# First edges of a GNN's nodes: 64 fixed rows of sorted destinations per window, marked and summed on TensorE, in place of a histogram and one row gather per window; edge gathers two for each finished one-hot

## The reference

```python
edge_index = jnp.stack([src, dst])              # 206250 edges, sorted by dst, 6250 nodes, 64 features
h = jnp.maximum(_layernorm(x), 0.0)
x = x + _L0_gnn_ref(h, edge_index, ...)         # two GIN convolutions
h = jnp.maximum(_layernorm(x), 0.0)
x = x + _L1_gnn_ref(h, edge_index, ...)         # message MLP, segment sum, update MLP

def _gin_conv(x, src, dst, Wa, ba, Wb, bb):
    agg = jax.ops.segment_sum(x[src], dst, num_segments=N)
    return jax.nn.relu((x + agg) @ Wa + ba) @ Wb + bb
```

## Time and profile before

| | |
|---|---|
| median of 3 runs | 957.7 us |
| profiled execution (its span) | 940.74 us (938.9 us) |
| PE busy | 873.5 us, 93% of the span |
| DVE busy | 699.8 us, 75% |
| ACT busy, POOL busy | 480.2 us, 401.3 us |
| `build` ends at | 386 us |
| indirect DMAs | 98, of which 49 are row gathers |

### The profile page before, as it was taken

The page is one execution under the profiler, slowest core; times in us unless marked ns, Lnnn a source line. Parts: engine busy times, 40 slices in busy tenths (PEclk is TensorE's granted clock), DMA queues, the critical chain, the costliest instruction groups (busy, mean ns, idle before and its releaser), DMA issues.

```text
span 938.9 us, 25210 instructions
## 1 busy us (share of the span) xinstructions
PE 873.5 (93%) x11282; PEld 709.5 (76%) x11282; DVE 699.8 (75%) x656; ACT 480.2 (51%) x573; POOL 401.3 (43%) x281
## 2 busy tenths in 40 slices
PE   0589999999999999899999999999999989999996
PEld 0258888988999999778777677777777867777774
DVE  7789999999999999384555555665545676778773
ACT  2655646554545554364545455445454455554551
POOL 5878888887000000304536656540010144454450
PEclk9969999999999999999999999999999999999998
DMA  3024344344333444315434334443442466788871
GB/s 111 18 87 132 106 154 152 106 135 152 109 123 123 140 140 140 134 34 163 121 114 130 110 116 121 134 125 105 124 119 63 138 200 204 238 233 242 244 215 48
DMA packets 81857, 126.86 MB, mean 135 GB/s; under 512 B 10288, under 2 KB 58544, under 8 KB 81616
## 3 DMA queue, kind: packets, MB, share of 16 engines
q1 hardware_dynamic: 78608, 121.98, 43.1%
q0 software_dynamic: 3136, 3.22, 1.5%
HBM read 84.22 MB, written 40.94 MB: 133 GB/s over the span
## 4 chain that ended last, share of the span: by engine, by line
PE 52%; DVE 4%; ACT 1%; issue 1%; POOL 0%; DVEq 0%; POOLq 0%; ACTq 0%
PE net_ps_hi L1271 15%; PE net_ps_lo L1271 14%; PE net_ps_lo L1288 7%; PE net_ps_hi L1288 7%; PE net_ps_mt L1214 5%; PE net_ps_ft L1214 2%; DVE net_wide L833 1%; PE net_ps_check L1306 1%; DVE hT L926 1%; DVE hT L921 1%; ACT net_wide L1110 1%; DVE net_first L933 1%; PE net_ps_mt L1318 0%; POOL net_wide L879 0%; PE net_ps_mt L1358 0%
## 5 line engine op out<-in xcount | busy, mean ns | idle before, releaser
L1271 PE MATMUL net_ps_hi<-net_wide,net_first 128*128 128x512 f32 (+1 forms) x637 | 248.4, 394 | 1.3 <-POOL net_wide L879 1.3
L1271 PE MATMUL net_ps_lo<-net_wide,net_first 128*128 128x512 f32 (+1 forms) x637 | 240.8, 382 | 0.0
L833 DVE CAST net_wide<-net_raw 128x3584 fp32r<-128x3584 uint8 (+1 forms) x90 | 202.4, 2257 | 42.1 <-PE net_ps_lo L1288 16.3
L1110 ACT ACTIVATE net_wide<-net_raw 128x3584 fp32r<-128x3584 uint8 (+1 forms) x64 | 193.6, 3025 | 78.1 <-PE net_ps_lo L1271 44.9
L338 DVE TENSOR_TENSOR build_hot_lo<-build_grid_lo,build_keys_t 128x4096 bf16<-128x4096 bf16 x100 | 225.1, 2283 | 2.9 <-PE build_ps_cnt L569 2.9
L589 PE MATMUL build_ps_out<-build_parts_pad,build_cnts 128*128 128x195 bf16 x2401 | 223.3, 250 | 2.8 <-ACT build_cnts L456 1.2
L456 ACT ACTIVATE build_cnts<-build_ps_cnt 128x980 uint16<-128x980 f32 (+3 forms) x176 | 151.3, 900 | 128.1 <-PE build_ps_cnt L569 125.6
L589 PEld LDWEIGHTS build_ps_out<-build_parts_pad,build_cnts 128*128 128x128 fp8e4 x2401 | 202.5, 98 | 8.5 <-issue 4.0
L1271 PEld LDWEIGHTS net_ps_hi<-net_wide,net_first 128*128 128x128 f32 x637 | 119.8, 188 | 31.8 <-issue 7.0
L1271 PEld LDWEIGHTS net_ps_lo<-net_wide,net_first 128*128 128x128 f32 x637 | 119.9, 188 | 24.7 <-issue 2.6
L833 POOL CAST net_wide<-net_raw 128x3584 fp32r<-128x3584 uint8 (+1 forms) x28 | 84.8, 3028 | 106.2 <-PE net_ps_hi L1288 52.5
(11 more groups left out here) (171 smaller groups left out, 709.2 us busy)
## 6 DMA issues: line engine op xcount, KB each, us to landing
net_raw<-edge_counts SPq DMA_DIRECT2D x168, 448.0 KB, 3.8
edge_counts<-build_cnts SPq DMA_DIRECT2D x168, 224.0 KB
xres<-in_x SPq DMA_DIRECT2D x1, 1568.0 KB, 7.1
net_raw<-edge_counts SPq DMA_DIRECT2D x14, 112.0 KB, 2.0
out<-xres SPq DMA_DIRECT2D x12, 128.0 KB, 4.2
build_rows<-in_dst_rows,build_row_i POOLq DMA_INDIRECT x49
build_edges<-in_edges,build_start_i POOLq DMA_INDIRECT x49
edge_counts<-build_cnts SPq DMA_DIRECT2D x7, 112.0 KB
```

Of the source, the lines that this page charges most:

```text
L833: return issue(expanded[e % WIDE_RING][:, 0:n, :, :].rearrange("p w a d -> p (w a d)"), raw[e % RAW_RING][:, 0:n, :, :].rearrange("p w a d ...
L1110: expand(act, lambda to, x: nc.scalar.activation(to, x, ACT.Identity), e).then_inc(grown["act"], 1)
L1271: last = nc.tensor.matmul(ps[(b + 1) % 2][:, 0:n * P], first[:, c, lo:lo + H], expanded[e % WIDE_RING][:, 0:n, k, :], start=(c == 0), stop ...
```

## The change

The host now also passes, for each window w, 64 rows of sorted destinations around row 33 w - 15 (`rows`), and the row ahead of each of them (`rows_before`). They are loaded by plain DMAs from SP, two of 32 KB for pair 0 and two of 768 KB for the other pairs; two windows lie on the two halves of the partitions. x is loaded by ACT's queue in four pieces. DVE marks which pivots a node has passed (`past`, bf16) and subtracts each row from the next (`jump`). PE multiplies the jumps by the marks, which adds up to the row in which the node's first edge lies less the node's own number (`select_rows`, L614 and L620), ACT takes the sign (`sign_rows`, L475), two matmuls of one column per window count (`rank_rows`, L631 and L632), and DVE adds the span's base (`find_starts`, L319). This goes in ten looks: one pair, two pairs, then three pairs each. All ten stand ahead of the first `count`.

All row gathers, the compares and the histogram are gone. The edge gather of window w waits, from w = 4 on, until (w - 3) / 2 one-hots, rounded up, are finished.

```diff
+def look(k):
+    if k < 2:
+        return (slice(0, 1), slice(1, LOOK))[k]
+    return slice(LOOK * (k - 1), min(LOOK * k, NU))
+def found_with(w):
+    return w // 2 // LOOK + 1 if w > 1 else 0
+def asked_behind(w):
+    return -(-(w - AT_ONCE + 1) // 2)
...
-                sp.dma_start(xin, a["x"].rearrange("p (w f) -> p w f", f=F)).then_inc(x_in, 16)
+                for i, u in enumerate((look(0), slice(1, NU))):
+                    sp.dma_start(span_rows[:, u, :], a["rows"].rearrange("p (u e) -> p u e", e=P)[:, u, :]).then_inc(span_in[i], 16)
+                    sp.dma_start(span_before[:, u, :], a["rows_before"].rearrange("p (u e) -> p u e", e=P)[:, u, :]).then_inc(span_in[i], 16)
...
+                def gather_edges(g, lo, hi):
                     for w in range(lo, hi):
-                        nc.gpsimd.indirect_dma_start(rows[:, w, :], None, a["dst_rows"],
-                                                     bass.IndirectOffsetOnAxis(ap=row_i[:, w:w + 1], axis=0)
-                                                     ).then_inc(rows_in[g], 16)
+                        if w == lo or found_with(w) != found_with(w - 1):
+                            pool.wait_ge(starts_known, found_with(w) + 1)
+                        if w >= AT_ONCE:
+                            pool.wait_ge(hot_ready, asked_behind(w))
...
+                def pass_pivots(u):
+                    shape = [P, u.stop - u.start, P // 2, 2]
+                    v.tensor_tensor(past[:, u, :].rearrange("p u (k t) -> p u k t", t=2),
+                                    grid_lo[:, :].rearrange("p (k t) -> p k t", t=2)[:, None, :, :].broadcast_to(shape),
+                                    piv_off[:, u, None, :].broadcast_to(shape), ALU.is_gt).then_inc(passed, 1)
+                def row_jumps(i, u):
+                    dve.wait_ge(span_in[i], 32)
+                    v.tensor_tensor(jump[:, u, :], span_rows[:, u, :], span_before[:, u, :], ALU.subtract).then_inc(jumps, 1)
+                def find_starts(k):
+                    u, turns = look(k), min(2, NW - 2 * look(k).start)
+                    by_pair = [t[:, :].rearrange("p (u t) -> p t u", t=2)[:, 0:turns, u] for t in (start_i, span_base)]
+                    dve.wait_ge(ranked, k + 1)
+                    v.tensor_tensor(by_pair[0], ps_start[k % CNT_RING][:, 0:turns, 0:u.stop - u.start], by_pair[1], ALU.add
+                                    ).then_inc(starts_known, 1)
...
+                def sign_rows(k):
+                    u = look(k)
+                    n, turns = u.stop - u.start, min(2, NW - 2 * u.start)
+                    act.wait_ge(selected, k + 1)
+                    nc.scalar.activation(sign[:, 0:turns, u, :], ps_cnt[k % CNT_RING][:, 0:turns, 0:n * P].rearrange("p t (u e) -> p t u e", e=P),
+                                         ACT.Sign, bias=half[:, 0:1]).then_inc(signed, 1)
...
+                for i, w in enumerate(shares):
+                    act.dma_start(xin[:, w, :], a["x"].rearrange("p (w f) -> p w f", f=F)[:, w, :]).then_inc(x_in[i], 16)
+                act.wait_ge(consts, 7)
+                nc.scalar.activation(warm[:, :], half[:, :], ACT.Sign)
+                for k in range(0, 3):
+                    sign_rows(k)
+                copy_first_keys(0)
+                for k in range(3, LOOKS):
+                    sign_rows(k)
                 for q, w in enumerate(shares):
                     act.wait_ge(centred, q + 1)
                     nc.scalar.activation(tmp[:, w, :], h64[:, w, :], ACT.Square).then_inc(squared, 1)
-                copy_first_keys(0)
-                compare_rows(1)
...
+                def select_rows(k):
+                    u = look(k)
+                    n = u.stop - u.start
+                    if k >= CNT_RING:
+                        pe.wait_ge(starts_known, k - CNT_RING + 1)
+                    if k == 5:
+                        pe.wait_ge(keys_copied, 1)
+                    pe.wait_ge(passed, 1 + (k > 0))
+                    turns = min(2, NW - 2 * u.start)
+                    for t in range(turns):
+                        nc.tensor.matmul(ps_cnt[k % CNT_RING][:, t, 0:n * P].rearrange("p (u e) -> p u e", e=P), lane_share[:, :],
+                                         grid_lo[:, None, :].broadcast_to([P, n, P]), start=True, stop=False)
+                    pe.wait_ge(jumps, 1 + (k > 0))
+                    for j in range(n):
+                        for t in range(turns):
+                            e = slice(t * ROWS, (t + 1) * ROWS)
+                            last = nc.tensor.matmul(ps_cnt[k % CNT_RING][:, t, j * P:(j + 1) * P], jump[e, u.start + j, :],
+                                                    past[e, u.start + j, :], start=False, stop=(j == n - 1))
+                    last.then_inc(selected, 1)
+                def rank_rows(k):
+                    pe.wait_ge(signed, k + 1)
+                    for w in range(2 * look(k).start, min(2 * look(k).stop, NW)):
+                        u, t = divmod(w, 2)
+                        e = slice(t * ROWS, (t + 1) * ROWS)
+                        to = ps_start[k % CNT_RING][:, t, u - look(k).start:u - look(k).start + 1]
+                        nc.tensor.matmul(to, sign[:, t, u, :], minus_half[:, :], start=True, stop=False)
+                        last = nc.tensor.matmul(to, past[e, u, :], row_step[e, :], start=False, stop=True)
+                    last.then_inc(ranked, 1)
...
+                for k in range(0, 3):
+                    select_rows(k)
+                    rank_rows(k)
+                pe.wait_ge(consts, 15)
                 turn_keys(0, first_keys[0]).then_inc(first_turned, 1)
+                for first in range(3, LOOKS, 3):
+                    for k in range(first, min(first + 3, LOOKS)):
+                        select_rows(k)
+                    for k in range(first, min(first + 3, LOOKS)):
+                        rank_rows(k)
...
+                pe.wait_ge(starts_known, LOOKS)
                 count_first(0, 2)
```

213 lines of the change are left out of this document (85 added, 128 removed).

## The result

The changed kernel has a median of 957.5 us over 20 runs (949.1 to 967.9), the kernel before one of 949.2 us over 20 (939.3 to 970.0). The ratio is 1.0108, 95% interval 1.0074 to 1.0142: slower, by about 10 us. That is clear of the noise, though under the 2% that the prediction took for the least that can be told. The ratio compares the undisturbed executions alone, so it is not quite that of the two medians. The forecast was no change. Its number, 957.5, is the measured median to 0.1 us, but by luck: it was the old median of 957.7 over three runs with nothing added, and over twenty runs that median is 949.2. As differences, the range of 8 in 10 was -9.5 to +9.5 us, and the measurement lies just outside. The profiled execution took 951.66 us, with a span of 949.3 us, against 940.74 and 938.9.

What follows compares the result with a forecast made beforehand. DVE's chain was taken to set the end of `build`: start 69.3 + steady part 291.2 + tail 24.6 = 385.1 us against 385.15, `net` unchanged. So the median was forecast at 957.5 us, with 8 in 10 from 948 to 967.

Steps and rivals of the forecast that it cites:

- What bounds the kernel: `build`: DVE's chain sets the end, 385.15 us before the change; PE is faster after the gathers and waits.
- rival B: Late parts of x: first `use` at 71.7, PE's chain ends at 389.2, 4 us slower, up to 10; chance 0.20.
- Steps 1 to 4: Start, first look to span 0's keys: first starts 8.3, second rows 13.5, `row_jumps` 1.7, keys done at 22.1 us.
- Steps 5 and 6: Start: means and centring, three looks' starts at 28.0, a one-hot quarter, looks 6 to 9 done at 34.0 us.
- T2: Start of pair 2's `hot_a` on DVE: forecast 69.3 us, 4.1 later than before (65.24).
- Steps 7 and 8: Start, from 34.0 to 69.3 us: squares, scaling, keys and one-hot quarters, with 2.0 of waiting for the keys' copy.
- The clock: PE in the start: 1.2 GHz granted from 54.8 to 65 us; no higher clock counted on from the added matmuls.
- The steady part's gain: DVE, pair 2 to 24: 295.27 less 2.9 of waits for PE and 1.2 of `find_starts` gives 291.2 us.
- Pacing at 0: Edge gathers' wait for one-hots: four gathers at 3.1 us at most, 12.4 us, costed at 0 on DVE.
- Rival D: Edge gathers' wait for one-hots starves DVE of edges: some 3 us, 5 spans, +10 to +15 us; chance 0.03.
- Rival A: Start: earlier rows, no wait for keys' copy, full clock; T2 at 64.1, 5.2 us faster, up to 9; chance 0.22.
- C: PE's loss is not the gathers': its chain keeps 324.1 us and ends at 389.1, 4 slower; chance 0.10.

Runs made afterwards that it cites:

- `ranks_grouped`: Changed kernel with each look's `sign` matmuls (128 rows of weights) first, then all `past` ones (64 rows): `build` ends at 382.1 us, ratio 1.0043.
- `ranks_tall`: Changed kernel with the second rank matmul also given 128 rows of weights, step 0 on the other window's rows: `build` ends at 384.1 us, ratio 1.0059.
- `changed_third`: The changed kernel unaltered, profiled on the same chip as the kernel before: `build` ends at 391.0 us, ratio 1.0139.

## Why the prediction was wrong

- **What bounds the kernel: right.** DVE sets the end in both kernels; PE's first `use` at 72.13 (as late as rival B had it, 71.7) held up no one-hot: no `hot_lo` waits for PE after 60 us, and what DVE waits for there is the copy of the keys (3.1 us) and the last sum.
- **Steps 1 to 4: right in the main.** The second rows were there at 13.46 (13.5), `row_jumps` took 1.68 (1.7). The first look was 1.7 us late (10.03 instead of 8.3), which cost nothing, since the second rows came later still. The keys were done 1.1 us late (23.2 instead of 22.1), behind two looks whose ranks DVE waited for.
- **Steps 5 and 6 failed.** "Three looks' starts: 28.0" was 31.5 and "done at 34.0" was 40.5. The term is the rank of a look. Step 6 prices it at 0.6 and names no row for it; twelve matmuls at the histogram's 0.055 us come to about that, and those have one height. It is 1.40, because heights alternate. `ranks_grouped` and `ranks_tall` take the alternation away and T2 falls to 66.9 and 68.4, near the forecast 69.3; on one chip it falls from 76.12 to 68.43, 7.7 us, against a miss of 7.1. The Trainium skill states the rule ("TensorEngine Tiling (Array Packing)", Key Properties: "Changing tiling mode (not just tile) drains the TensorE"). These runs agree with it, at 0.09 us a change; and six matmuls of 64 rows that change between the two halves, but not in height, start within 0.16 us in `ranks_grouped`.
- **Steps 7 and 8: right in size.** They were priced at 35.3 us from 34.0 to T2 and took 35.9 from 40.5; the wait for the keys' copy was 3.1, not 2.0.
- **The clock: as counted.** The prediction counted on no higher clock in the looks, and by the 0.58 us of the 448-column matmul at 50.82 there was none.
- **The steady part's gain was a property of one profile.** 290.76 was forecast at 291.2, so the number is right. But the 4.1 us that it was to give back, of which 2.9 were waits for a late PE, are not there on quieter chips: the kernel before has 291.12 too. There the whole loss of the start shows (11.8 us), while the two first profiles show 7. With short ranks the time is still 0.3 to 0.6% above the kernel before. That is about the start's own forecast loss of 4.1 us with nothing to pay for it. A term read from one execution was taken as one of the kernel.
- **Pacing at 0** held on one chip, and was wrong by 27 us on another, on the side of the change: without it GpSimd's queue would have run free as soon as all starts were known. Rival D had its sign wrong; DVE never waits for edges after 70 us.
- Rival A did not occur. Of C the cost did not occur; that PE's loss is not simply the gathers' is borne out, since with all 98 of them PE's stops at counts fall from 7.4 to 1.4 us in another execution. B's time lay nearest (4 to 10 us slower, where 10 were measured), by another mechanism.

## What to carry to other kernels

Price a small matmul from a row in which the row height of the weights changes as it will in the new code; count the changes of height, group them away, or pad the short side with zeros. A chain PE to ACT to PE to DVE of many small looks costs its full length where DVE's queue holds nothing between them. Before a gain is counted that comes from an engine's unexplained stops, see whether another execution of the same kernel has them. Check a printed clock against a matmul whose time is known at both levels.

## What the runs showed of the hardware

- A one-column matmul follows the one before in 0.027 us when both have 128 rows of weights (`ranks_tall`), and in 0.117 us when 128 and 64 alternate (the changed kernel). Both at 1.2 GHz: the 384-column fills take 0.82 us for two in both, and 0.50 in `ranks_grouped`. In `changed_third` the alternating ones are 0.108 us apart from 35.0 to 38.3 us, just before the granted clock falls (0.59 from 38 to 40 us), and 0.117 before and behind; if that is the higher level, as I read it, the price of a change hardly depends on it.
- Gathers issued every 1.25 us were met by a stop of PE of 19.5 us on one chip and by none on another, with the same program. In the first execution the ranks from 35 to 39 us were not stopped beside gathers at that pace (PE is busy 9.54 of 10 us from 30 to 40), while the counts from 42 to 48 us were, up to 1.17 us at a time. No instruction load of the core's queue q8 starts between 42.1 and 88.3 us there, where the other execution has one at 62.1. That PE waited for its instructions is a guess, and it goes on at 84.13, ahead of the next load; no run here shows what held it.
